# Windowed-attention layers: values by 32x32-block transposes and per-head products with x, in a new instruction order

## The reference, cut to what matters

```python
for i in range(DEPTH):                                   # 6
    x = attn_layer(shift_tokens(x), Wqkv[i], ..., Wo[i]) + x
    x = ffn_layer(shift_tokens(x), ln_g[i], ..., b2[i]) + x
# attn_layer, per window and head:
#   q, k = rotary(l2norm(x @ Wq)), rotary(l2norm(x @ Wk)); v = x @ Wv
#   attn = softmax(mask(8 * q @ k.T)); out = attn @ v    (64 keys: the window before, its own)
#   result = concat over 16 heads of out, @ Wo
```

## Time and profile before

| what | value |
|---|---|
| median of three runs | 2051.35 us |
| span of the profiled execution | 2050.9 us |
| TensorE busy | 2008.4 us (98%) |
| VectorE, ScalarE, GpSimd busy | 73%, 70%, 71% |
| mean granted TensorE clock | 0.993 |
| DMA | 206.96 MB, 37.5% of 16 engines' span |

### The profile page before, as it was taken

The page is one execution under the profiler, slowest core; times in us unless marked ns, Lnnn a source line. Parts: engine busy times, 40 slices in busy tenths (PEclk is TensorE's granted clock), DMA queues, the critical chain, the costliest instruction groups (busy, mean ns, idle before and its releaser), DMA issues.

```text
span 2050.9 us, 60046 instructions
## 1 busy us (share of the span) xinstructions
PE 2008.4 (98%) x23046; PEld 1248.5 (61%) x23046; DVE 1493.8 (73%) x3296; ACT 1425.8 (70%) x2704; POOL 1455.4 (71%) x1436
## 2 busy tenths in 40 slices
PE   8999999999699999999999999999999999999998
PEld 5555555555465666666666666666666666666655
DVE  5666666666687787777787777877777877777763
ACT  5666666665367777777677777777777777776774
POOL 3344443433688888888987888888888788878872
PEclk9999999999799999999999999999999999999999
DMA  4000000000355554445644554544654446445451
GB/s 137 6 1 12 1 7 6 6 1 4 106 131 143 141 152 120 114 123 149 162 107 120 133 156 131 131 122 112 168 140 112 125 126 173 114 120 138 110 128 50
DMA packets 219130, 206.96 MB, mean 101 GB/s; under 512 B 32482, under 2 KB 211680, under 8 KB 218720
## 3 DMA queue, kind: packets, MB, share of 16 engines
q1 hardware_dynamic: 218848, 203.14, 37.5%
HBM read 84.58 MB, written 14.68 MB: 48 GB/s over the span
## 4 chain that ended last, share of the span: by engine, by line
PE 66%; ACT 5%; issue 3%; DVE 1%; POOL 0%; DMA 0%; SPq 0%; ACTq 0%; DVEq 0%; POOLq 0%
PE bank L938 17%; PE bank L1050 15%; PE bank L1151 9%; PE bank L1079 6%; PE bank L1288 5%; PE bank L1126 5%; PE bank L972 3%; PE bank L1310 3%; ACT L985 1%; PE bank L1171 1%; ACT U L1057 1%; ACT GE L1294 1%; PE bank L1262 1%; PE bank L907 1%; ACT LG L985 0%
## 5 line engine op out<-in xcount | busy, mean ns | idle before, releaser
L1050 PE MATMUL bank<-WU,XT 128*32 128x512 f32 x3072 | 414.4, 599 | 4.7 <-ACT U L1057 1.4
L938 PE MATMUL bank<-XT,WQK 128*128 128x256 f32 x1520 | 391.5, 391 | 15.1 <-DVE T L959 9.2
L683 POOL TENSOR_SCALAR PR<-PR,RI 128x512 f32<-128x512 f32 x256 | 174.0, 694 | 292.3 <-DVE RI L570 291.1
L964 POOL TENSOR_TENSOR T<-T 128x512 f32<-128x512 f32 x288 | 362.6, 1283 | 24.5 <-DVE T L959 24.4
L1016 POOL TENSOR_TENSOR T<-T,RB 128x512 f32<-128x512 f32 x288 | 361.6, 1294 | 2.0 <-DMA RB<-norms 1.9
L1116 POOL TENSOR_TENSOR PL<-PL,RIL 128x512 f32<-128x512 f32 x192 | 199.3, 1050 | 218.9 <-DVE RIL L1109 218.9
L938 PEld LDWEIGHTS bank<-XT,WQK 128*128 128x128 f32 x1520 | 269.6, 192 | 106.7 <-issue 42.1
L489 ACT ACTIVATE PR<-PR,NM 128x512 f32<-128x512 f32 x256 | 183.5, 718 | 165.5 <-DVE NM L565 164.4
L1057 ACT ACTIVATE U<-bank 128x512 f32<-128x512 f32 x384 | 227.0, 591 | 74.9 <-PE bank L1050 74.3
L944 ACT ACTIVATE SQ<-bank 128x512 f32<-128x512 f32 x380 | 225.8, 594 | 67.0 <-PE bank L938 67.0
L959 DVE TENSOR_TENSOR T<-bank,TAB 128x512 f32<-128x512 f32 x380 | 258.8, 681 | 0.0
(11 more groups left out here) (148 smaller groups left out, 3462.7 us busy)
## 6 DMA issues: line engine op xcount, KB each, us to landing
RB<-norms SPq DMA_DIRECT2D x384, 128.0 KB, 3.1
QP<-T SPq DMA_DIRECT2D x192, 256.0 KB, 4.9
KZ<-T1F SPq DMA_DIRECT2D x192, 128.0 KB, 3.0
KZ<-T SPq DMA_DIRECT2D x192, 128.0 KB, 2.9
TAB<-rotary_dram SPq DMA_DIRECT2D x24, 512.0 KB, 5.9
norms<-RN SPq DMA_DIRECT2D x95, 128.0 KB, 1.7
WQK<-wqk_halves_dram SPq DMA_DIRECT2D x12, 512.0 KB, 5.4
WVS<-wv_turned_dram SPq DMA_DIRECT2D x29, 128.0 KB, 2.6
```

The source lines that it names most:

```text
L938: m = pe.matmul(b[:, ab * HALF:(ab + 1) * HALF], WQK[n % 3][:, i, ab, :], XT[s % 2][:, hf * HALF:(hf + 1) * HALF], start=True, stop=True)
L964: pool.tensor_tensor(t1, t1, T2[i % 2][:, ::-1, :], ALU.add).then_inc(l_rotated.sem, 1)
L1050: i = pe.matmul(bank[1][h * WIN:(h + 1) * WIN, :], XT[s % 2][:, c0:c0 + WIN], WU[:, lp * HG + h, :], start=True, stop=True)
```

## The change

For a tile, VectorE now turns the probabilities itself, in 32x32 blocks, in two instructions (`dve_turn_probs`). `pe_heads` multiplies them by x: for each of four windows and two key windows, a 32x128 block of keys' x is stationary and 32x512 turned probabilities (16 heads by 32 queries) move; the four windows lie in four row groups of the array and go to banks 2, 3, 1 and 4. ScalarE keeps the four results (`act_keep_heads`, 128x512 each). `pe_out` then makes 16 products of 128x128 by 128x128, one for a head, summed in bank 7. The keys' x (XS) and the same moved by one window (XP) are copied by five DMAs for a step (`sp_keys`, `sp_back`). Scores and results of heads share banks 2 and 3, so `pe_heads` of tile k-1 waits until VectorE has shifted both halves of tile k. Because bank 4 is now in use, the guess lies in the SBUF tile LG, and Newton's intermediate in SM. XN2 shares memory with XNT2. The slots are written in a new order.

```diff
-            guess = bank[4][:, HALF:SEQ]
+            guess = LG[:, :]
@@ dve_newton
-                dve.scalar_tensor_tensor(Y2[:, :], guess, -0.5, SM[:, :], ALU.mult, ALU.mult).then_inc(l_newton.sem, 1)
+                dve.scalar_tensor_tensor(SM[:, :], guess, -0.5, SM[:, :], ALU.mult, ALU.mult).then_inc(l_newton.sem, 1)
...
-                dve.tensor_tensor(Y2[:, :], guess, Y2[:, :], ALU.mult).then_inc(l_newton.sem, 1)
+                dve.tensor_tensor(SM[:, :], guess, SM[:, :], ALU.mult).then_inc(l_newton.sem, 1)
...
-                dve.scalar_tensor_tensor(RN[:, :], Y2[:, :], 1.5, guess, ALU.add, ALU.mult).then_inc(l_newton.sem, 1)
+                dve.scalar_tensor_tensor(RN[:, :], SM[:, :], 1.5, guess, ALU.add, ALU.mult).then_inc(l_newton.sem, 1)
@@ removed: pe_u, act_keep_u, pe_turn_probs, act_keep_probs, pe_values; added:
+            def dve_turn_probs(s, t, half):
+                dve.wait_ge(l_probs_normed.sem, l_probs_normed.at(g, half))
+                dve.wait_ge(l_heads_done.sem, l_heads_done.at(g - 1))
+                v = PL[half][:, :].rearrange('p (k h j) -> p k h j', k=2, h=8)
+                dve.transpose(PT[:, :, 8 * half:8 * half + 8, :], v).then_inc(l_probs_turned.sem, 1)
+            hbank = [bank[2], bank[3], bank[1], bank[4]]
+            def pe_heads(s, t):
+                pe.wait_ge(l_probs_turned.sem, l_probs_turned.at(g))
+                pe.wait_ge(l_heads_kept.sem, l_heads_kept.at(g - 1))
+                if g + 1 < TOTAL:
+                    pe.wait_ge(l_shifted.sem, l_shifted.at(g + 1))
+                pe.wait_ge(l_clamped.sem, l_clamped.at(min(g + 4, FRONTS - 1)))
...
+                for k, keys in enumerate((XP[s % 2], XS[s % 2])):
+                    for w in range(4):
+                        r = slice(w * WIN, (w + 1) * WIN)
+                        m = pe.matmul(hbank[w][:, :], keys[r, t, :], PT[r, k, :, :].rearrange('p h q -> p (h q)'), start=k == 0, stop=k == 1)
...
+            def act_keep_heads(s, t, w):
+                act.wait_ge(l_heads_done.sem, l_heads_done.at(g, w))
+                act.wait_ge(l_y_done.sem, l_y_done.at(g - 1))
+                act.activation(YS[:, :, w * WIN:(w + 1) * WIN], hbank[w][:, :].rearrange('p (h q) -> p h q', h=HEADS), ACT.Copy).then_inc(l_heads_kept.sem, 1)
+            def pe_out(s, t):
...
+                pe.wait_ge(l_heads_kept.sem, l_heads_kept.at(g))
+                for h in range(HEADS):
+                    lane, i = h % HG, h // HG
+                    m = pe.matmul(bank[7][:, 0:E], YS[:, h, :], WU[:, lp * HG + lane, i * E:(i + 1) * E], start=h == 0, stop=h == HEADS - 1)
@@ pe_square_sums
-                pe.wait_ge(l_probs_kept.sem, l_probs_kept.at(f - 4))
+                pe.wait_ge(l_heads_kept.sem, l_heads_kept.at(f - 5))
@@ act_mask
+                act.wait_ge(l_heads_kept.sem, l_heads_kept.at(g - 2, half))
```

More of the change, by code:

```diff
@@ L220, in pe_ln_turn @@
                 else:
[L221 removed]
+                    pe.wait_ge(s_c, 5)
                 for t in range(TPB):
@@ L1040, in act_boundary @@
                 act.activation(KZ[1][:, :, :, 0:WIN], KZ[0][:, :, :, HALF:HALF + WIN], ACT.Copy).then_inc(l_boundary.sem, 1)
[L1042 to L1057, removed]
             def act_mask(s, t, half):
@@ L1143, in pe_values @@
-                for gg in range(2):
-                    for k in range(2):
-                        for w in range(4):
-                            if t + w + k == 0:
-                                continue
-                            u = U6[(4 * g + w - 1 + k) % 6]
-                            grp = 2 * half + gg
-                            first = half + gg == 0 and (k == 0 or t + w == 0)
-                            i = pe.matmul(bank[7][w * WIN:(w + 1) * WIN, 0:E], PTL[half][:, 2 * k + gg, w * WIN:(w + 1) * WIN], u[:, grp * E:(grp + 1) * E], start=first, stop=half + gg + k == 3, skip_group_check=True)
@@ L1424, in pe_slot @@
                     pe_front(k + 4, 1)
+                if step_at(k - 6, LAST - 1):
+                    pe_ffn_turn((k - 6) // 4)
+                if step_at(k - 7, LAST - 1):
+                    pe_ffn_up((k - 7) // 4, 2)
+                if half_at(k + 5):
+                    pe_turn_x((k + 5) // 2)
+                if here(k - 1):
+                    pe_heads(*tile(k - 1))
+                if step_at(k - 7, LAST - 1):
+                    pe_ffn_up((k - 7) // 4, 3)
+                if new_f(k + 4):
+                    pe_front(k + 4, 2)
+                    pe_front(k + 4, 3)
@@ L1485, in act_slot @@
+                if here(k - 1):
+                    act_keep_heads(*tile(k - 1), 3)
+                if new_f(k + 4):
+                    act_square(k + 4, 3)
+                if here(k + 1):
+                    act_mask(*tile(k + 1), 0)
+                if half_at(k + 5):
+                    act_keep_xt((k + 5) // 2)
                 if here(k):
-                    act_keep_u(*tile(k), 0)
                     act_exp(*tile(k), 1)
                 if new_f(k + 4):
-                    act_square(k + 4, 0)
@@ L1491, in dve_slot @@
-            def dve_slot(k):
+                    act_guess(k + 4)
+                if here(k + 1):
+                    act_mask(*tile(k + 1), 1)
+                if step_at(k - 1, LAST):
+                    act_next_vo((k - 1) // 4)
+                if step_at(k - 6, LAST - 1):
+                    act_ffn_gelu((k - 6) // 4, 0)
+                if step_at(k - 5, LAST - 1):
+                    act_ffn_scale((k - 5) // 4)
+                if step_at(k - 6, LAST - 1):
+                    act_ffn_gelu((k - 6) // 4, 1)
@@ L1516, in dve_slot, with pool_slot @@
                 if here(k):
                     dve_max(*tile(k), 0)
-                if half_at(k + 4):
-                    dve_keep_xt((k + 4) // 2)
+                    dve_max(*tile(k), 1)
+                    dve_shift(*tile(k), 0)
+                    dve_shift(*tile(k), 1)
+                if new_f(k + 4):
+                    dve_products(k + 4, 0)
+                    dve_products(k + 4, 1)
+            def pool_slot(k):
+                if new_f(k + 3):
+                    pool_rotate(k + 3, 2)
+                if change_at(k + 4, 4):
+                    pool_fold_scale(*divmod(k + 4, 16))
+                if new_f(k + 3):
+                    pool_rotate(k + 3, 3)
+                if new_f(k + 4):
+                    pool_rotate(k + 4, 0)
+                    pool_rotate(k + 4, 1)
+                if here(k):
+                    pool_normalise(*tile(k), 0)
+                if hold_f(k + 3):
+                    pool_scale(k + 3, 0)
@@ L1592, in pe_layers_program @@
             def pe_layers_program():
-                for k in range(-7, TOTAL + 2):
+                for k in range(-7, TOTAL + 3):
                     pe_slot(k)
@@ L1631, in pool_layers_program @@
                 pool.sem_inc(l_folded.sem, 4)
-                for k in range(-7, TOTAL + 2):
+                for i in range(2):
+                    pool.memset(XS[i][0:1, 0, DH:E], 0.0).then_inc(s_edge, 1)
+                    pool.memset(XP[i][0:WIN, 0, :], 0.0).then_inc(s_edge, 1)
+                for k in range(-7, TOTAL + 3):
                     pool_slot(k)
```

303 lines of the change are left out of this document (126 added, 177 removed).

## The result

The changed kernel takes **2203.7 us** (median of four runs, 2200.38 to 2210.58), the kernel before 2051.02 on the same chip: a ratio of **1.0746**, 95% interval 1.0733 to 1.076. The forecast was 2146 us, with a range of 2010 to 2215. The profiled execution spans 2198.6 us, 147.7 more than the 2050.9 of before.

A forecast was written before the change was run, and what follows sets the result against it. TensorE bound the kernel before at 15.57 us a slot; the new loop's 16.05, with extras, made 16.55, so +90 us over 92 slots and +5 at the end: 2050.9 + 95 = 2146 us, range 2010 to 2215.

The forecast's parts named there:

- Newton: VectorE's three chained instructions, now reading two SBUF operands, each wait out a GpSimd pass: 3.9 us, bounds 1.6 and 5.0.
- the four scalings and the late addition: Trace evidence for waiting on GpSimd: scalings 3.01 us beside GpSimd adds against 1.1 without; an add 1.67 for 0.69.
- The loop: Once a slot through heads, ScalarE's copies and square, VectorE's products to shifts: 12.15 + 3.9 = 16.05 us.
- TensorE's waits ahead of heads: TensorE would show idle time before heads, released by VectorE's shift, of 1 to 2.5 us a slot.
- cost nothing unless they hold it up: SyncE's queue: five more DMAs for a step, issued three slots ahead of use behind the relayout, priced at nothing.
- the upper end: Top of the forecast's own range, 2205 us, from Newton's bounds and from 3.6 to 4.3 us for `pe_out`.
- keep their length: The last four tiles, without fronts, stay as long as before; only the very end adds 5 us.
- rival 1: Newton meets GpSimd rarely or briefly; a loop of 13.95 us through ScalarE's copies and squares binds: 2033 us, 14%.
- the rival of 3.84: Four row groups do not share, heads take 3.84 us inside the loop: +177, 2320 us; 8% with a turn waiting for GpSimd.
- the turn: VectorE's turning of probabilities: two added a slot, 0.61 us each, bounds 0.3 and 1.9 if it waits for GpSimd.
- TensorE's own work: Per slot 5.6 us added and 6.4 removed, falling by 0.85 us to 14.7 us.
- rival 2: TensorE stays the bound, its other pieces filling both gaps: 14.7 us a slot, 1976 us, 11%.

The follow-up runs named there:

- e1: Changed kernel with only the guess moved back from SBUF to PSUM bank 4: 2087.41 us, ratio 1.017 to the kernel before.
- e4: Kernel before with only the guess moved from bank 4 to the SBUF tile LG: 2156.33 us, ratio 1.0505.
- e2: Changed kernel with only SyncE's load of the rotary tables issued two slots earlier: 2168.65 us, ratio 1.058 to the kernel before.
- e3: Changed kernel with both edits, guess in bank 4 and tables two slots earlier: 2048.5 us, ratio 0.9979 to the kernel before.
- e7: e5 with ScalarE's copy of the turned x put ahead of the mask: 2031.55 us, ratio 0.991 to the kernel before.
- e5: e3 with heads' banks reordered and ScalarE's squares ahead of the last two copies of heads: 2043.71 us, ratio 0.9963 to the kernel before.

## Why the prediction was right, and where it fell short

- **Sign and mechanism: right.** Newton was priced at 3.9 us with its guess, and 3.38 + 0.25 = 3.6 was found. Each instruction waits out a GpSimd pass, as argued from the four scalings and the late addition. The Trainium skill says the same (SBUF — State Buffer, Who interferes with whom, of a VectorE instruction with two SBUF inputs); this case's trace agrees, with 234 of 249 ending right behind such a pass. e1 and e4 give it a price here: 3.38 us in place of 1.27 for three instructions, 105 to 120 us in 96 fronts. GpSimd's passes lengthened too, though by less than the 0.3 allowed: its normalise from 1050 ns to 1125, as the groups of that stretch have it.
- **A step: near, but by two errors.** The loop was priced at 16.05 us for every plain slot, and it binds in two of four: TensorE's waits ahead of heads are 50.9 + 29.8 = 80.7 us for the 82 slots of the stretch, 1.0 a slot, at the low edge of the 1 to 2.5 forecast. An undisturbed step takes 64.2 to 64.6 us against 66.2. But only 3 of after's 23 steps, cut at the scores of tiles 0, 4, 8 and so on, are that short; the others take 65.0 to 75.3. With the tables early (e2) sixteen slots take 260 to 267 us, on average 264, the forecast's 4 x 66.2 = 265 and not 4 x 64.4 = 258. In e3 sixteen slots take 245, next to 4 x 60.8 = 243. So these long slots came with Newton's length; how the meeting with GpSimd varies from slot to slot wasn't taken apart. The fit with 265 is in part luck: the forecast had no long steps and put the short ones too high.
- **The step that failed** is the sentence that SyncE's additions "cost nothing unless they hold it up". It counted the DMAs that were added and not the ones that moved, and so the sum had no term for the tables. The tables' load moved by two slots to the slot of its use, and that is 35 us alone (e2) and 39 behind e1 (2087.4 - 2048.5). It is the larger part of the 57.7 us by which the forecast fell short. That 2203.7 still lies in the forecast's own range of 2095 to 2205 is luck: the upper end stood for a longer Newton and a dearer `pe_out`, and neither was found.
- **Also missing: the end.** The last four tiles "keep their length", with +5 for the very end, came out at +12.9, and +12.5 in e3. Without the fronts the tiles there are a chain through heads, four copies and `pe_out`, with only pieces of the feed-forward beside it. PE in order of time there, and the engines' row of the stretch behind the wait (its clock is the number before the last two):

```profile
2119.45 2.09 PE L1126 MATMUL bank<-PT,XP 32*128 32x512 f32 x8 [4.15 <-DVE PL L1081]
2121.28 1.96 PE L1126 MATMUL bank<-PT,XS 32*128 32x512 f32 x8
```

```profile
2121.30:2123.20 1.90, 1.90 (x13) 0.40 (x5) 0.00 (x0) 0.00 (x0) 1.35 (x2) 0.50 1.04 214
```

Behind a wait of 4.15 us for VectorE's shift, heads take 1.83 us from start to start in place of 0.96, at a granted clock of 0.50, the 1.2 GHz level; that adds 1.8 us for the eight products. The end as a whole is 8 us of the miss, and half of the 15 by which e3 lies above rival 1's 2033.
- **The sum of the misses**, within the profiled execution (147.7 us where the sum said 95): 35 tables, 8 at the end, -1 at the start, and the other 11 in the 92 slots. These 11 are again a difference: 23 steps of 64.4 us would lie 33 us under the forecast's 1424.4 + 90 for the 92 slots, and the long slots that the tables don't explain put 44 on top. Part of that is TensorE's clock, which no term of the sum stood for: from 600 to 1900 us it was granted at 0.98 after and at 1.00 in e3 and e7. The median lies 5 us over the profiled span, and makes up the 57.7.
- **Heads share fully.** Eight products in four row groups cost 1.92 us, as taken; the rival of 3.84 is out. The Trainium skill (TensorE: Matmul & The Clock Gate, Part 3, measured speedup) has 3.07 times, by which it would be an estimated 2.4 us; in this case's trace it is four times, since one product takes 0.95. `pe_out` 3.77 for 3.65, the turn 0.61 to 0.63 from start to start, as taken, and it doesn't wait for GpSimd.
- **Rivals 1 and 2.** TensorE's own work was priced right: 14.8 us a slot in e3 and e7, for 14.7. That TensorE is the bound, as rival 2 has it, comes true in e7, with slots of 15.0 us. Its time of 1976 us does not (2031.55): a step falls by 62.3 - 60.0 = 2.3 us and not by 3.5, and the end is longer. The terms of rival 1's loop add up to 13.90 and not 13.95, which is 0.2 us a step and changes nothing.
- **What was wrong of the runs' expectations:** e4 above all. It held the cost of a longer VectorE in a kernel bound by TensorE to be small, from average shares. e1's put all of the gain into the undisturbed step, and e5's did not look for the wait next in line.

## What to carry to other kernels

An elementwise instruction of VectorE with two operands in SBUF waits out the GpSimd pass that is under way, here 0.5 to 0.9 us on top of 0.42; one operand in PSUM is enough to avoid it, so look at where operands lie before a bank is given to something else. When an order is rewritten, write down for each load how many slots lie between its issue and its first reader, before and after; here a load of 4.9 us cost 35 us in the slot of its use, and two slots earlier it left waits of 7.0 us. Before an instruction is made longer on an engine with time to spare, look for the results behind it in its list and how long their readers can wait: half a microsecond of room decided e4. When a wait is taken away and the gain is small, the wait that took its place names the next swap: here one of two lines on ScalarE gave 12 us.

## What the runs showed of the hardware

- The 32x32 block transpose of 128x512 float32 took 692 ns, like other passes of that size, from SBUF to SBUF; it isn't held up by a running GpSimd pass (1234.02, above), while the 128x256 `scalar_tensor_tensor` with two operands in SBUF right before it is.
- A VectorE instruction with two operands in SBUF took 0.42 us beside an idle GpSimd and ended some 0.3 us behind the GpSimd pass that it met. It is not always let in between two passes: in e4 one (L991, 881.32 us) took 4.49 us, through the rest of a scale, one more scale and two additions.
- Four row groups with 32 rows and 512 columns ran in the time of one product: 0.96 us for eight records, where a single product has 0.95 for two.
- The same three waits cost about as much in the kernel before, where TensorE hardly waited, as in the kernel after: 105 and 116 us.
